# Mamba layers of a fused cross-attention kernel: each silu in two halves, two gates two units sooner, and one product with C per pair

## The reference

```python
xz = jnp.einsum('bsd,ed->bse', x, ip_w)
xi, z = jnp.split(xz, 2, axis=-1)
conv = causal depthwise conv of xi over time, 4 taps, + cb
xi = jax.nn.silu(conv)
dt, Bm, Cm = jnp.split(xi @ xp_w.T, [16, 32], axis=-1)
dt = jax.nn.softplus(dt @ dtp_w.T + dtp_b)
dA = jnp.exp(dt[..., None] * -jnp.exp(A_log))
dBu = dt[..., None] * Bm[:, :, None, :] * xi[..., None]
h = da * h + dbu                      # one step of the scan over time
y = einsum(h, C) + xi * Dp
y = y * jax.nn.silu(z)
h_out = h_in + y @ op_w.T             # with an rmsnorm ahead of each layer
```

## Time and profile before

| | us |
|---|---|
| median of 3 runs | 6636.77 (6634.72 to 6638.04) |
| the profiled execution, its own time | 6639.8 |
| its span | 6638.0 |
| span of the 36 Mamba bodies (first scan to last) | 2054.0 to 5993 |
| DVE busy in the span | 4928.1 (74%) |
| PE busy in the span | 6129.0 (92%) |
| POOL busy in the span | 4394.1 (66%) |
| ACT busy in the span | 3620.5 (55%) |

### The profile page before, as it was taken

How to read it: one execution, slowest core, us unless ns; L and a number is a source line. 1 busy time by engine, 2 the same in 40 slices (tenths; PEclk the granted TensorE clock), 3 DMA queues, 4 the chain that set the end, 5 groups by cost and what they waited for, 6 DMA issues and landing times. The chain is left out here.

```text
span 6638.0 us, 60681 instructions
## 1 busy us (share of the span) xinstructions
PE 6129.0 (92%) x20586; PEld 2577.4 (39%) x20586; DVE 4928.1 (74%) x5709; ACT 3620.5 (55%) x6605; POOL 4394.1 (66%) x2056
## 2 busy tenths in 40 slices
PE   9999999999999989898899989898989898988898
PEld 4555555544443333323333323333323343323444
DVE  4444445543225999999999999999999999995623
ACT  4444445432225666666666666666666666664432
POOL 3333334323005999999999999999999999992300
PEclk9999999999998989899989999999999898989998
DMA  2000000213002333333333333332333232332000
GB/s 80 1 1 1 1 1 1 86 26 102 20 0 68 83 76 78 78 93 85 72 89 71 83 88 86 71 89 65 89 81 93 65 89 65 93 80 56 4 0 26
DMA packets 228678, 387.64 MB, mean 58 GB/s; under 512 B 46304, under 2 KB 64416, under 8 KB 225936
## 3 DMA queue, kind: packets, MB, share of 16 engines
q1 hardware_dynamic: 228368, 383.75, 23.7%
HBM read 207.14 MB, written 23.40 MB: 35 GB/s over the span
## 5 line engine op out<-in xcount | busy, mean ns | idle before, releaser
L2506 POOL TENSOR_TENSOR work<-work,weights 128x1024 f32<-128x1024 f32 x1152 | 2685.6, 2361 | 15.8 <-PE banks L2384 6.8
L2429 DVE TENSOR_TENSOR_SCAN banks<-banks,work 128x512 f32<-128x512 f32 x1584 | 1985.7, 1272 | 53.5 <-ACT banks L2474 48.1
L2384 PE MATMUL banks<-work 128*64 128x512 f32 x4608 | 1353.9, 670 | 378.2 <-POOL work L2511 271.1
L2474 ACT ACTIVATE banks<-work 128x512 f32<-128x512 f32 x2304 | 1496.0, 680 | 25.5
L1992 PE MATMUL banks<-work,weights 128*128 128x512 f32 (+31 forms) x3796 | 1140.6, 451 | 3.0 <-DVE work L2222 3.0
L2237 DVE TENSOR_TENSOR work<-banks,weights 128x512 f32<-128x512 f32 x1584 | 1056.0, 668 | 0.0
L2511 POOL TENSOR_TENSOR work<-work,weights 128x1024 f32<-128x1024 f32 x360 | 848.0, 2356 | 238.4 <-ACT work L2129 238.4
L2429 DVE TENSOR_TENSOR_SCAN work<-banks,work 128x512 f32<-128x512 f32 x720 | 911.2, 1269 | 99.8 <-ACT banks L2474 97.2
L603 POOL TENSOR_TENSOR work<-work 128x1024 f32<-128x1024 f32 x256 | 479.6, 1893 | 743.4 <-DVE work L470 742.9
L1992 PEld LDWEIGHTS banks<-work,weights 128*128 128x128 f32 x3796 | 634.4, 190 | 600.0 <-issue 523.6
L2133 ACT ACTIVATE work<-banks 128x2 f32<-128x2 f32 x792 | 135.9, 172 | 1227.4 <-DVE work L2237 1225.6
(11 more groups left out here) (312 smaller groups left out, 6796.9 us busy)
## 6 DMA issues: line engine op xcount, KB each, us to landing
weights<-mamba_bc SPq DMA_DIRECT2D x592, 256.0 KB, 5.0
work<-work SPq DMA_DIRECT2D x1160, 128.0 KB, 2.3
weights<-mamba_taps SPq DMA_DIRECT2D x5, 2048.0 KB, 7.5
weights<-cross_vo SPq DMA_DIRECT2D x16, 512.0 KB, 6.9
mamba_taps<-work SPq DMA_DIRECT2D x4, 2048.0 KB, 7.8
cross_vo<-weights SPq DMA_DIRECT2D x6, 1024.0 KB, 8.4
work<-in_conv_rows SPq DMA_DIRECT2D x16, 256.0 KB, 6.7
out_T<-X SPq DMA_DIRECT2D x8, 512.0 KB, 3.3
```

Source lines behind the costliest of these rows:

```text
L2384: mm = e.matmul(ybank[k % 2][64 * h:64 * h + 64, :], fold, ring_pair(n, j)[:, h, :], start=False, stop=(a == SP_ - 1))
L2429: e.tensor_tensor_scan(ub if by_pool(j) else da, da, ub, state[:, i:i + 1], ALU.mult, ALU.add).then_inc(scanned, 1)
L2474: e.activation(banks[:, slot_of(i), :], dt_rep[:, k % 2, h, :], ACT.Exp, scale=decay[:, f:f + 1]).then_inc(da_full, 1)
L2506: e.tensor_tensor(ring_pair(n, j), u_rep[:, k % 2], bc[:, a, 0, :].unsqueeze(1).to_broadcast([P, 2, TC]), ALU.mult) \
```

## The change

Four things are edited. Silu of z and silu of xi are each cut in two halves of 128x1024 (two channel groups each): z behind units 5 and 27 (pairs 2 and 13), xi behind units 15 and 21 (pairs 7 and 10), with two table loads around each half. The drain of E3 goes from unit 13 to 15, and the two steps of the rstd from units 21 and 23 to 23 and 24. The gates of k = 0 and 1 go from units 23 and 39 to 21 and 37; those at 7 and 55 stay, and the gates of k = 0 and 2 wait for the z half that they read. `times_c` makes one product of 128x1024 for both units of a pair, behind the first scan of the next pair. Besides, `times_x` on POOL leaves out a small instruction in the one chunk in nine without a batch boundary, and SP waits for E3's drain ahead of loading the next layer's first weights.

```diff
@@ late_pe
-            e.wait_ge(silu, val(N, 2, 4))
+            e.wait_ge(silu, val(N, 4, 7))
@@ tables
-    E_OUT, G_OUT, F_OUT, SILU_AT = (59, 3, 9, 13), 29, (55, 49, 33, 1), (15, 7)
+    E_OUT, G_OUT, F_OUT = (59, 3, 9, 15), 29, (55, 49, 33, 1)
+    Z_SILU, X_SILU = (5, 27), (15, 21)
+    GATE_AT = (21, 37, 55)
@@ late_act
-        if i == SILU_AT[1]:
...
-            e.activation(zn, zn, ACT.Silu).then_inc(silu, 1)
-            e.preload_act_table_set("natural_log_exp_and_others")
-        if i == SILU_AT[0]:
...
-            e.activation(xi, xi, ACT.Silu).then_inc(silu, 1)
-            e.preload_act_table_set("natural_log_exp_and_others")
+        for half in range(2):
+            at = slice(2 * half, 2 * half + 2)
+            if i == Z_SILU[half]:
...
+                e.activation(zn[:, at, :], zn[:, at, :], ACT.Silu).then_inc(silu, 1)
+                e.preload_act_table_set("natural_log_exp_and_others")
+            if i == X_SILU[half]:
+                if half == 0:
+                    e.wait_ge(ln.v_free, v_at(previous(N), "E1"))
+                else:
+                    e.wait_ge(ln.v_free, v_at(N, "E3"))
+                    e.wait_ge(ln.s_free, s_at(previous(N), "E2"))
+                e.activation(xi[:, at, :], xi[:, at, :], ACT.Silu).then_inc(silu, 1)
+                e.preload_act_table_set("natural_log_exp_and_others")
-    SQUARE_AT, RSTD_AT, SCALE_AT = 5, (21, 23), 26
+    SQUARE_AT, RSTD_AT, SCALE_AT = 5, (23, 24), 26
@@ gate
-        if k == 0:
-            e.wait_ge(silu, val(N, 2, 3))
+        if k % 2 == 0:
+            e.wait_ge(silu, val(N, 4, (5, 8)[k // 2]))
@@ times_c
-    def times_c(e, N, n, j, h):
-
-        i = 2 * j + h
-        last = e.tensor_tensor(ring_pair(n, j)[:, h, :], banks[:, slot_of(i), :], bc[:, j % SP_, 1, :], ALU.mult)
-        if h == 1:
-            last.then_inc(prod_d, 1)
+    def times_c(e, N, n, j):
+
+        e.wait_ge(scanned, scanned_at(N, 2 * j + 1))
+        e.tensor_tensor(ring_pair(n, j), banks[:, slot_of(2 * j):slot_of(2 * j) + 2, :], bc[:, j % SP_, 1, :].unsqueeze(1).to_broadcast([P, 2, TC]), ALU.mult) \
+            .then_inc(prod_d, 1)
@@ vector
-                            if i == 16 * (f + 1) + 7:
+                            if i == GATE_AT[f]:
...
                         if h == 0 and j > 0 and not by_pool(j - 1):
-                            e.wait_ge(scanned, scanned_at(N, i - 1))
-                            times_c(e, N, n, j - 1, 1)
-                        if h == 1 and not by_pool(j):
-                            e.wait_ge(scanned, scanned_at(N, i - 1))
-                            times_c(e, N, n, j, 0)
+                            times_c(e, N, n, j - 1)
```

More of the change, by code:

```diff
@@ L2161, in late_act @@
             e.activation(xi[:, 3, :], lane_v, ACT.Identity, bias=lv("conv_b", 3)).then_inc(ln.v_free, 1)
-        if i == SILU_AT[1]:
[L2163 to L2167, removed]
-            e.activation(zn, zn, ACT.Silu).then_inc(silu, 1)
-            e.preload_act_table_set("natural_log_exp_and_others")
-        if i == SILU_AT[0]:
-            e.wait_ge(ln.v_free, v_at(N, "E3"))
-            e.wait_ge(ln.s_free, s_at(previous(N), "E2"))
-            e.activation(xi, xi, ACT.Silu).then_inc(silu, 1)
-            e.preload_act_table_set("natural_log_exp_and_others")
+        for half in range(2):
+            at = slice(2 * half, 2 * half + 2)
+            if i == Z_SILU[half]:
+                if half == 0 and N[1] >= 0:
+                    e.wait_ge(y_free, y_free_at(previous(N), "F1"))
+                    e.wait_ge(ln.v_free, v_at(previous(N), "F0"))
+                if half == 0 and N[1] < 0:
+                    e.wait_ge(cleared, 1)
+                if half == 1 and N[1] >= 0:
+                    e.wait_ge(y_free, y_free_at(N, "F3"))
+                e.activation(zn[:, at, :], zn[:, at, :], ACT.Silu).then_inc(silu, 1)
[8 more added lines that the diff above has]
+                e.preload_act_table_set("natural_log_exp_and_others")
         for m in range(KD):
@@ L2251, in times_x @@
         at = slice(2 * pair, 2 * pair + 2)
-        e.tensor_tensor(u[:, at, :], dt[:, at, :], xi[:, at, :], ALU.mult).then_inc(u_done, 1)
+        p = reset_of(c)
+        e.tensor_tensor(u[:, at, :], dt[:, at, :], xi[:, at, :], ALU.mult).then_inc(u_done, 2 if p is None else 1)
+        if p is None:
+            return
         e.wait_ge(u_done, u_done_at(N, pair, 1))
-        p = reset_of(c)
-        e.tensor_tensor(scrap[:, 12:14] if p is None else dt[:, at, p], far, core.one[:, 0:2], ALU.mult).then_inc(u_done, 1)
+        e.tensor_tensor(dt[:, at, p], far, core.one[:, 0:2], ALU.mult).then_inc(u_done, 1)
     def build_diag(e):
@@ L2430, in _ @@
                         if h == 0 and j > 0 and not by_pool(j - 1):
-                            e.wait_ge(scanned, scanned_at(N, i - 1))
-                            times_c(e, N, n, j - 1, 1)
-                        if h == 1 and not by_pool(j):
-                            e.wait_ge(scanned, scanned_at(N, i - 1))
-                            times_c(e, N, n, j, 0)
+                            times_c(e, N, n, j - 1)
                         if h == 1 and j == PAIRS_N - 1 and not by_pool(j):
-                            e.wait_ge(scanned, scanned_at(N, i))
-                            times_c(e, N, n, j, 1)
+                            times_c(e, N, n, j)
             N = (LAYERS // 2, 0)
```

## The result

The changed kernel takes 6675.7 us (5 runs, 6671.4 to 6676.6) against 6636.9 (5 runs): the ratio is 1.0057, 95% interval 1.0044 to 1.0070. It is 38.8 us slower, where the forecast was +10.5 and the range ended at 6672. The sign and the way it comes about were forecast; the size was not.

A forecast was written before the change was run, and what follows sets the result against it. A closed chain through DVE, POOL and PE was taken as the bound, 109.14 us a body against 108.92: +7.7 us over 35 distances, +2.8 ahead of the first body, together +10.5, so 6647 us; range 6617 to 6672.

The forecast's parts named there:

- The closed chain: DVE from unit 21 to 41, POOL, PE's 49.59 us stretch, back to unit 21: 109.14 us a body against 108.92.
- The gate at 21: At unit 21 the k = 0 gate waits for pair 7's fold on PE, about 0.6 us a body.
- the list of silus: Delays behind half silus on ACT: 1.7 us at pair 2, 1.2 at pair 7, covered at pairs 10 and 13.
- The product: DVE's one 128x1024 multiply per pair: next start after 1.14 us against 1.18 for two small ones, 0.04 saved a pair.
- rival B: Thin bank handover behind the large product makes each DVE-multiplied pair's scan wait: 110.7 us a body, 6703 us; chance 0.15.
- the softplus: Behind pair 22 it holds ACT for 3.9 us; without the next half product as cover, DVE waits 0.6 us.
- The half silus: Each half holds ACT 3.65 us against 4.52 for a whole; DVE waits 1.7 us at pair 2, 1.2 at pair 7.
- rival C: A half silu holds ACT as long as a whole, 4.52 us: at most 112.0 us a body, 6748 us; chance 0.05.
- Rival A: DVE's own chain decides, the gate finds pair 7's fold done: body 108.5 or 108.0 us, 6617 us; chance 0.23.
- Ahead of the first body: Silu of xi precedes the projection to dt, B and C; two halves of 3.65 for 4.52 add 2.8 us once.
- DVE's own body: DVE's body if nothing else stops it: 104.9 + 0.1 + 3.5 = 108.5 us, 0.4 less than before.

The follow-up runs named there:

- one tie left: Changed kernel with B0's drain behind unit 22, gate at 21 (6646.9 us; with two small products 6658.8), or drain at 19, gate at 23, two small products (6684.3).
- PE was out of the way: Changed kernel with B0's drain behind unit 22 and the k = 0 gate at unit 23: 6630.4 us with the large product, 6585.5 with two small ones.

## Why the prediction was wrong

- **The closed chain** from unit 21 over POOL, PE and back is right: 1.83, 23.5 and 49.58 us are the medians in the changed kernel and in those with one tie left.
- **The gate at 21** is right in mechanism and in size: 0.66 us from the end of the fold to the scan (0.64 forecast). In the changed kernel it waits only 0.16 us, since the scan of unit 20 ahead of it has already waited 1.06 us for ACT.
- **The step that failed** is in the list of silus: "pair 10: the gate, 0.59, now stands in between and covers it". It gave ACT 7.4 us from pair 8's last scan to pair 11's first, as if ACT were free. It is not: the drain of B0 stands between, at unit 19, and waits 1.2 us for PE, at a time fixed by PE's stretch. From the scan of unit 17 to that of unit 22 it takes 9.87 us. The trace of before had that wait, 0.46 us a body, and the prediction did not list it. The chain fold of pair 26, B0, drain, exponentials, half silu, exponentials, unit 22 is 0.8 us longer than that of the gate: unit 21 to 41 took 34.42 and not 33.6. With the drain moved it took 33.57 and the kernel 6646.9 us. How much of this reaches the time hangs on the product: moving the drain gives back 29 us with the large product and 6 with two small ones.
- **The product** was sized slightly low in gain (0.06 a pair, not 0.04). It was right that normal pairs wait for nothing, which disposes of rival B as written (a wait at every pair). It was wrong to count the lost cover at only one place, the softplus (0.6; 0.8 measured as a distance of 1.99 for 1.18). Wherever ACT is late for another reason, DVE has half a product less to do meanwhile. That made the product a loss of 11 us in the changed kernel and of 45 once PE was out of the way; only with the gate alone on the path was it the gain that was forecast.
- **The half silus**: the wait at unit 6 was 1.4 (1.7 forecast), at unit 16 1.2 (1.2). Table loads cost their 1.28 and no more, 3.67 us for a half: rival C did not come. Rival A, the faster one, would have needed PE earlier, and PE was not.
- **Ahead of the first body**: +2.1 for +2.8.

- **DVE's own body** was put at 108.5 us, 0.7 too long: with the drain moved the gate waits 1.33 us in a body of 109.20 and not 0.6. The product's next start at 1.12 and not 1.14 makes 0.4 of it, the shorter wait at unit 6 most of the rest. It cost the forecast nothing, since the gate's wait takes up the difference, but the gate's own wait and the faster rival were sized by it.

Of the 38.8 us the late drain of B0 gives back 29 by the medians, and 32 if each kernel is set against the kernel before of its own group. The rest, +7 to +10, agrees with the forecast of +10.5.

## What to carry to other kernels

List every wait of the engine that feeds the bound, its drains included, ahead of placing more work on it: a wait of 0.4 us that is off the path becomes part of it as soon as a long instruction is put behind it. When two engines meet at several places in a loop, look for every tie between them, since removing one shows little while another of about the same length is left. Merging two instructions saved 0.06 us a pair here, but it also took away the small work that had filled the time in which another engine was late. Which of the two is larger changed sign here with the place of two other instructions.

## What was not expected of the hardware

The product of 128x1024 takes 1.203 us in the mean here (1.192 to 1.226), with the second input read twice, against 1.225 for the one near the end of the kernel; the row of the changed kernel's groups:

```profile
L2246 DVE TENSOR_TENSOR work<-banks,weights 128x1024 f32<-128x1024 f32 x792 | 952.6, 1203 | 1.2
```

The next instruction starts 1.12 us behind its start, so the one product saves 0.06 us against two small ones.
